# Delta memory: the products of last keys and queries, eight pairs in one run per group

## The reference, cut to what matters

```python
def _fast_weight_memory(q, k, v, beta):        # per batch entry and head
    def step(W, xs):
        qt, kt, vt, bt = xs
        v_old = einsum('bhij,bhj->bhi', W, kt)
        W = W + (bt * (vt - v_old))[..., :, None] * kt[..., None, :]
        return W, einsum('bhij,bhj->bhi', W, qt)
...
q = elu(q) + 1; k = elu(k) + 1                 # then each divided by its sum over the head
denom_acc = cumsum(k, axis=2)
denominator = einsum('bhld,bhld->bhl', denom_acc, q)
```

## Time and profile before

| | |
|---|---|
| time, median of 3 runs | 988.71 us (988.32 to 990.34) |
| span of the profiled execution | 993.1 us |
| time of the profiled execution itself | not given beside its span |
| PE busy | 926.8 us (93%) |
| DVE busy, ACT busy, POOL busy | 544.1, 543.1, 365.3 us |
| keys and queries of groups 0, 1, 2, 3 (first L1802 to last L1824) | 456.8 to 502.6, 515.3 to 566.6, 609.9 to 655.6, 702.4 to 748.9 us |

### The profile page before, as it was taken

One profiled execution on the slowest core, in us unless ns is written; L12 is line 12 of the kernel. 1 busy time (PEld: TensorE's weight loads), 2 busy tenths in 40 slices (PEclk: granted clock), 3 DMA queues, 4 the chain that ended last, 5 costly groups with the idle time before them and its releaser, 6 DMA issues.

```text
span 993.1 us, 31589 instructions
## 1 busy us (share of the span) xinstructions
PE 926.8 (93%) x11919; PEld 693.9 (70%) x11919; DVE 544.1 (55%) x1934; ACT 543.1 (55%) x1082; POOL 365.3 (37%) x387
## 2 busy tenths in 40 slices
PE   7999999999999999969998899999999999999990
PEld 6446655664689999965544594577458589999990
DVE  5236455355476532207579648767786787861104
ACT  2543343325305555536766666775678476666760
POOL 2300412321234776543140112122432345777760
PEclk9999999999999999989999999999999999999995
DMA  8744314403403233213020120120015513133316
GB/s 220 225 88 86 70 48 100 108 24 89 105 28 82 77 96 94 64 60 129 3 87 3 51 83 1 46 89 16 22 55 162 163 30 82 56 98 96 105 37 254
DMA packets 78260, 82.77 MB, mean 83 GB/s; under 512 B 12207, under 2 KB 60164, under 8 KB 77600
## 3 DMA queue, kind: packets, MB, share of 16 engines
q1 hardware_dynamic: 64128, 58.29, 22.3%
q0 software_dynamic: 10176, 19.04, 6.2%
q10 hardware_dynamic: 3808, 3.41, 1.1%
HBM read 53.96 MB, written 27.64 MB: 82 GB/s over the span
## 4 chain that ended last, share of the span: by engine, by line
PE 32%; DVE 11%; issue 4%; DMA 3%; ACT 3%; SPq 1%; POOL 1%; DVEq 0%; POOLq 0%; ACTq 0%
PE b_ring L1802 8%; PE b_ring L1745 4%; PE b_g L1851 4%; PE b_g L1824 4%; PE b_ring L1303 4%; PE b_ring L1314 4%; PE b_ring L1866 2%; DVE b_kq L2221 2%; ACT early L1979 1%; DMA early<-expert_parts 1%; DVE x L1391 1%; DVE b_prod L2130 1%; ACT b_outT L1991 1%; DVE b_coef L2133 1%; PE b_s L1811 1%
## 5 line engine op out<-in xcount | busy, mean ns | idle before, releaser
L1802 PE MATMUL b_ring<-b_hT,b_qkT 128*128 128x512 f32 x256 | 119.9, 607 | 6.0 <-DVE b_kq L2221 4.6
L2221 DVE SCALAR_TENSOR_TENSOR b_kq<-b_exp,b_ring 128x512 f32<-128x512 f32 x128 | 83.3, 683 | 40.2 <-ACT b_exp L1959 38.6
L276 POOL DMA_INDIRECT expert_rows<-f_route_sent,f_route_place_id x64 | 62.9, 982 | 97.4 <-DVE f_route_place_id L232 50.8
L1959 ACT ACTIVATE b_exp<-b_ring 128x512 f32<-128x512 f32 x128 | 73.8, 603 | 31.5 <-PE b_ring L1802 21.6
L1802 PEld LDWEIGHTS b_ring<-b_hT,b_qkT 128*128 128x128 f32 x256 | 45.3, 189 | 61.3 <-issue 41.0
L982 ACT ACTIVATE phik<-a_ring 128x512 f32<-128x512 f32 x64 | 38.2, 597 | 81.4 <-PE a_ring L825 81.4
L276 POOL DMA_INDIRECT expert_rows<-g_route_sent,g_route_place_id x48 | 50.0, 1041 | 83.7 <-PE b_ring L1866 36.9
L1303 PE MATMUL b_ring<-b_v,b_kq 128*128 128x128 f32 x568 | 75.3, 276 | 0.6 <-issue 0.4
L1303 PE MATMUL a_ring<-phik 128*128 128x128 f32 x568 | 75.0, 275 | 0.4 <-ACT phik L1324 0.4
L1314 PE MATMUL b_ring<-wide,b_v 128*128 x568 | 75.1, 276 | 0.0
L1314 PE MATMUL a_wide<-wide,phiqT 128*128 x568 | 74.7, 275 | 0.0
(11 more groups left out here) (332 smaller groups left out, 1838.2 us busy)
## 6 DMA issues: line engine op xcount, KB each, us to landing
a_rn_wide<-norm_compact SPq DMA_DIRECT2D x28, 512.0 KB, 8.4
wide<-in_L_ffn_W SPq DMA_DIRECT2D x32, 256.0 KB, 5.4
early<-expert_parts SPq DMA_DIRECT2D x12, 512.0 KB, 5.9
a_rn_wide<-expert_rows SPq DMA_DIRECT2D x71, 65.0 KB
b_coef<-gram_compact SPq DMA_DIRECT2D x4, 1024.0 KB, 4.9
b_hT<-expert_rows SPq DMA_DIRECT2D x56, 65.0 KB
x<-in_L_attn_a_x SPq DMA_DIRECT2D x8, 256.0 KB, 4.0
gram_compact<-wide SPq DMA_DIRECT2D x32, 64.0 KB
```

The lines of the kernel that those rows point to most:

```text
L276: pool.indirect_dma_start(self.rows, bass.IndirectOffsetOnAxis(self.place_id[:, k, n:n + 1], 0), self.sent[:, n, k, :], None).then_inc(sel ...
L1802: pe.matmul(ring[n % 4][:, :], w, hT[:, g % 2, half * 512:half * 512 + 512], start=True, stop=True)\
L1959: act.activation(exps[:, n % EXPS, :], ring[n % 4][:, :], ACT.Exp, bias=-1.0).then_inc(S["exp_ready"], 1)
L2221: dve.scalar_tensor_tensor(out=kq[:, p % 2, half:half + FOURS // 2, slot:slot + T * FOUR], in0=exps[:, n % EXPS, :].rearrange("p (a n) -> ...
```

## The change

The operands of the products no longer lie in two slots of a tile of their own but in eight rows, one for each pair. The rows lie in memory that is idle at that time: in `mix_tok` for group 0 and in the second half of `early` (the second slot of `spread`) for groups 1 to 3. GpSimd therefore no longer waits for `gram_done` before it writes one. On TensorE `products(p)` contains only the Gram matmuls for p < 7; at p = 7 the products of all eight pairs are done in one run ahead of the last Gram matmuls, with the waits for GpSimd and VectorE moved there. VectorE, which overwrites a slot of `kq` that GpSimd reads, gets a wait for `last_paired` at the start of pairs 2 to 7 (before, it was covered by `gram_done`).

```diff
-        last_pair = K.sb(ctx, "b_last_pair", [P, 2, P])
...
+        pair_rows = [rows.rearrange("p (q n) -> p q n", n=P) for rows in
+                     (mix_tok[:, :, :, :].rearrange("p a t h -> p (a t h)"), spread_flat[:, 2 * HD:2 * HD + PAIRS * P])]
...
+        def last_pair(g, p):
+            return pair_rows[min(g, 1)][:, p, :]
...
                 pool.wait_ge(S["kq_ready"], 4 * n + 4)
-                if n >= 2:
-                    pool.wait_ge(S["gram_done"], n - 1)
...
-                pool.tensor_tensor(last_pair[:, p % 2, :].rearrange("p (a b) -> p a b", b=FOUR),
+                pool.tensor_tensor(last_pair(g, p).rearrange("p (a b) -> p a b", b=FOUR),
...
+                def last_products():
+                    for p in range(PAIRS):
+                        if p < PAIRS - 1:
+                            pe.wait_ge(S["last_paired"], (PAIRS - 1) * g + p + 2)
+                        else:
+                            pe.wait_ge(S["pair_ended"], g + 1)
+                        for j in range(4):
+                            pe.matmul(s_bank[32 * j:32 * j + 32, 256:288], C["head_ind"][:, p, :],
+                                      quarter(last_pair(g, p), j, 1), start=(p == 0), stop=(p == PAIRS - 1),
+                                      skip_group_check=True)
+
                 def products(p):
-                    if p < PAIRS - 1:
-                        pe.wait_ge(S["last_paired"], (PAIRS - 1) * g + p + 2)
-                    else:
-                        pe.wait_ge(S["pair_ended"], g + 1)
-                    for j in range(4):
-                        pe.matmul(s_bank[32 * j:32 * j + 32, 256:288], C["head_ind"][:, p, :],
-                                  quarter(last_pair[:, p % 2, :], j, 1), start=(p == 0), stop=(p == PAIRS - 1),
-                                  skip_group_check=True)
+                    if p == PAIRS - 1:
+                        last_products()
+                    elif g == 0 and p == 0:
+                        pe.wait_ge(S["last_paired"], 1)
...
                     if k == 0 and p >= 2:
                         wait_apart(dve, S["gram_done"], g * PAIRS + p - 1, K.passed)
+                        dve.wait_ge(S["last_paired"], (PAIRS - 1) * g + p)
```

More of the change, by code:

```diff
@@ L2208, in end_pair @@
                 key, query = KEYS + (T - 1) * FOUR, QUERIES + (T - 1) * FOUR
-                dve.tensor_tensor(last_pair[:, 1, :].rearrange("p (a b) -> p a b", b=FOUR),
+                dve.tensor_tensor(last_pair(g, PAIRS - 1).rearrange("p (a b) -> p a b", b=FOUR),
                                   kq[:, 1, :, key:key + FOUR], kq[:, 1, :, query:query + FOUR], ALU.mult)\
```

## The result

The changed kernel takes 993.64 us (median of 19 runs, 989.41 to 997.76), the kernel before beside it on the same chip 990.34 us (19 runs, 988.07 to 994.34): ratio 1.003, with a 95% interval of 1.0018 to 1.0042. It is slower by 0.3%, where 987.9 us and "no change that can be told" were forecast; 993.64 also lies above the stated 985.2 to 991.2. Of the 5.7 us between 987.9 and 993.64, 1.6 are the base: the forecast was counted from 988.7, the median of 3 runs, and 19 runs have 990.34. The change itself was forecast at -0.8 us and measured at +3.3.

A forecast was written before the change was run, and what follows sets the result against it. PE, busy 93% of the span, was taken to bound most of the changed stages, VectorE much of group 1. Terms -4.2 + 2.5 + 0.3 + 0.6 = -0.8 us gave 987.9 us from the 988.7 median, range 985.2 to 991.2.

The forecast's parts named there:

- What bounds the kernel now: Four changed stages: PE mostly bounds, VectorE much of group 1; 25 of 32 product blocks on the chain.
- What is removed: PE's rounds: 21 product blocks on the chain save 0.20 us each, 4.2 us, at the least 1.3.
- Rival 4: PE's rounds: emptying moves to L1802/L1824, so nothing happens; +1.5 us, 990.2 us; chance 0.13 together with rival 2.
- What is added: Run at pair 7: 28 blocks come back at 11 ns a record, 2.5 us; 0.83 us for each run.
- Rival 2: Run at pair 7: a product costs 25 ns, as alone; +1.7 us, 990.4 us; chance 0.13 together with rival 4.
- The new wait on VectorE: Start of pairs 2 to 7: never holds, costs its own instruction, 0.3 us; above, 1.2.
- Instructions that come late: Ends of groups 1 and 2: instruction-fetch stalls shift more than grow; 0.3 us each, 0.6 in all.
- The prediction's own sign of being wrong: "Issue" gaps behind groups 1 and 2 differing from 2.04 and 1.90 us by more than half a microsecond.
- Rival 3: Ends of groups 1 and 2 starve for 112 more instructions; +3.8 us, 992.5 us; chance 0.15.
- Its clock: After group 1's 2.04 us stall PE runs at 0.50 clock, 568 to 572 us; a longer gap can lengthen this.

The follow-up runs named there:

- e3: Changed kernel with each pair's products back beside the pair, keeping the eight rows, VectorE's wait and GpSimd without its wait: 990.38 us, 0.9997 to the kernel before.
- e1: The kernel before, unchanged, run again: 990.53 us, ratio 0.9994 to the kernel before.
- e2: The changed kernel, unchanged, run again: 992.25 us, ratio 1.0017 to the kernel before.
- e5: Changed kernel with the products of pairs 0 to 6 left out on TensorE, their waits kept: 999.57 us, 1.0098 to the kernel before.
- e6: Changed kernel with the run of all eight pairs' products done twice: 1005.95 us, 1.0156 to the kernel before.
- x5: Changed kernel with 16 do-nothing counts on TensorE in each of seven rounds a group, four behind each projection matmul: 996.83 us, 1.0064 to the kernel before.
- e4: Changed kernel with the products of pairs 0 to 6 in one run ahead of the two value projections: 992.82 us, 1.0015 to the kernel before.
- x4: Changed kernel with two runs of four pairs, at pairs 3 and 7: 1057.01 us on a slower chip, 1.0018 to the kernel before there.
- x6: Changed kernel with 24 do-nothing counts a round, six behind each projection matmul: 1004.93 us, 1.0126 to the kernel before.
- p1: Kernel before with 128 waits and counts on TensorE ahead of the memory's first transpose, shifting packet borders: 1013.93 us, 1.0251 to the kernel before without shift.

## Why the prediction was wrong, point by point

- **"What bounds the kernel now"** held: the time taken out of PE's rounds was on the chain, and group 1 turned out to be VectorE's, as the earlier trace rows said.
- **"What is removed"**: 0.20 us a block held exactly (round 5.05). Rival 4, the emptying moving to the next border of shapes, is excluded: the Gram block follows L1804 after 3.63 us.
- **"What is added"**: 0.73 us for the run against 0.83 predicted; the 56 records more than in a block cost 0.53 us (0.73 - 0.20), 9.5 ns each against 11; 4 x 0.53 = 2.1 us against 2.5. Rival 2 is excluded. So is, for this shape, the rule of the Trainium skill, "TensorE: Matmul & The Clock Gate", "The mechanism", as the prediction read it, with an estimated 52 ns.
- **"The new wait on VectorE"**: e3 finds nothing (0.9997), against 0.3.
- **"Instructions that come late"** is the step that failed. I charged 0.6 us, "a choice near the lower bound", at two places; the runs show +7.2 us from e1 to e2, of which 3.0 are hidden in group 1, and +7.2 as the mean of four places, where little or nothing is hidden at three. Two reasons behind the choice were wrong. Only the ends were priced (3.3 us more in the mean), while the rounds, called lighter, gained 3.6 us of gaps. And "I expect stalls to shift more than to grow" had no row behind it: the average pace of 23 ns an instruction says nothing of a packet that begins about 2.4 us before its first instruction is needed, in a stretch that uses 256 in 1.42 us. The prediction's own sign of being wrong was there: behind group 2 the gaps are 1.66 and 1.63 us together where one of 1.90 stood. Behind group 1 it was not (2.32 for 2.04).
- The page "Runtime: NRT & Kernel Launch", "Instruction fetch mechanics", of the Trainium skill, by which a 16 KiB crossing is mostly hidden, spoke for the low price. Gaps of up to 2.8 us at these borders, 8 to 19 us of a kernel, disagree with it.
- **Rival 3** had the sign and, by chance, the size (992.5 against 993.6), with a chance of 0.15; its +3.8 us stand against a measured +3.3. Its mechanism is only in part right: e5 has long gaps at the ends without the 112 instructions, and the long gaps of the rounds, where it saw none, are as much of the loss. Its clock is no part of the +1.7 us from e1 to e2, whose mean granted clock from 490 to 800 us is 0.99 in both: 568 to 572 us stood at 0.50 in the first trace of the changed kernel, as in the earlier trace rows, and at 1.00 in that of e2, behind the same gap of 2.32 us (last section). Where gaps are more and longer (e6, x5) the clock is a part.

What is shown: the loss is idle time of PE at borders of its instruction packets; it comes with the move of the products, not with the operands; it is there in all four places of the borders that were tried. What stays open: why this order of instructions meets its packets later. The number of instructions in the last burst (e4, e5, x4) and the border's pace through the Gram block (x5) each explain a part at most. No run shows what makes a packet begin: it begins somewhere between 44 instructions ahead of the border before its own and its own border, and the shortest distance between two was 3.3 us.

## What to carry to other kernels

Where a stretch of small matmuls uses its instructions at some 5 ns each, look at "issue" gaps and count TensorE's instructions up to them: if they end at one place in every 256, the stretch is bound by the arrival of instructions, and taking out or bunching short work can cost more than it saves. Then the price of a move is not the sum of its durations; give such a term a range of several us and a good chance, and time the order itself. Gaps in a stretch that another engine bounds are free, so put the densest instructions there.

## What the runs showed of the hardware that was not expected

- Two executions of one kernel have their border gaps at the same instructions, yet runs of one kernel lie up to 8 us apart (989.41 to 997.76). One chip took 1055.19 us for what others did in 990.
- The granted clock behind the same gap differs between two executions of one kernel, 0.50 (1.2 GHz) and 1.00 (2.4 GHz). Busy time by engine in a window (PE, PEld, DVE, ACT, POOL), then the clock; first the first trace of the changed kernel, then e2:

```profile
568.00:572.00 4.00, 3.35 (x52) 3.04 (x45) 3.17 (x4) 3.46 (x8) 2.72 (x5) 0.50 0.28 79
```

```profile
568.00:572.00 4.00, 2.95 (x68) 2.76 (x70) 2.20 (x4) 3.29 (x7) 3.68 (x7) 1.00 0.42 119
```

- A bare count on TensorE is free between long matmuls (x5: four behind each matmul of 512 columns) and dear where PE has been idle. In the kernel before, PE stands idle for 8.32 us ahead of the memory; 64 counts put there began the first L1792 8 us later, 192 counts 29 us (455.2 in e1, 463.3 and 484.0 us): 0.13 to 0.15 us each. One reading fits both, though no run tests it: a count always takes that long and is hidden only while a matmul is still running. Six behind each matmul (x6) would be 0.9 us, as much as the matmul (3.63 / 4), and there the rounds begin to grow. 128 waits and counts made this gap (timeline of PE, p1):

```profile
470.83 1.94 PE L1740 MATMUL b_ring<-ident,b_h 128*128 128x128 f32 x8 [20.22 <-issue]
```
